# Mixture-of-experts tiles in the order of their first token's batch, with the closing norm of each batch run among the tiles

## What is computed

```python
x = x + layernorm(attention(layernorm(x)))            # x: (8, 512, 128)
# second layer: small 16-head attention, then 8 experts, 2 per token
x2  = h + attn16(rmsnorm(h)) @ w_up                   # h = layernorm(x)
t   = rmsnorm(x2)
w, idx = top2(softmax(t @ router_w))                  # idx: 2 of 8 experts
y   = sum_k w[k] * ((silu(t @ w1[e_k]) * (t @ w3[e_k])) @ w2[e_k])
out = x + layernorm(x2 + y)
```

## Time and profile before

| | us |
|---|---|
| median of 3 runs | 778.08 (777.09 to 778.49) |
| profiled execution | 779.29 |
| its span, first to last instruction | 777.3 |
| PE busy | 660.4 (85%) |
| DVE busy | 503.1 (65%) |
| ACT busy | 396.0 (51%) |
| POOL busy | 355.9 (46%) |
| mean granted TensorE clock | 0.95 |

### The profile page before, as it was taken

One profiled execution on the slowest core, in us unless ns is written; L12 is line 12 of the kernel. 1 busy time (PEld: TensorE's weight loads), 2 busy tenths in 40 slices (PEclk: granted clock), 3 DMA queues, 4 the chain that ended last, 5 costly groups with the idle time before them and its releaser, 6 DMA issues.

```text
span 777.3 us, 15273 instructions
## 1 busy us (share of the span) xinstructions
PE 660.4 (85%) x4861; PEld 394.9 (51%) x4914; DVE 503.1 (65%) x1623; ACT 396.0 (51%) x792; POOL 355.9 (46%) x398
## 2 busy tenths in 40 slices
PE   7976899999899799899989988979879799999900
PEld 3434456466466456546646644545534366666600
DVE  7465866968968677786876876766715144444456
ACT  3243376566476467456646635544521265655515
POOL 4150290391582566349147351640134155555565
PEclk9999799999999999999989999999989999999955
DMA  6101001001001000000100100100025332322163
GB/s 179 43 0 28 1 1 29 1 1 31 27 1 28 29 2 21 29 8 1 35 22 1 28 30 2 29 28 2 1 87 142 71 82 77 82 76 72 51 240 94
DMA packets 38008, 33.27 MB, mean 43 GB/s; under 512 B 6384, under 2 KB 33072, under 8 KB 37920
## 3 DMA queue, kind: packets, MB, share of 16 engines
q1 hardware_dynamic: 33616, 23.39, 11.3%
q0 software_dynamic: 4320, 8.92, 3.5%
HBM read 17.09 MB, written 12.01 MB: 37 GB/s over the span
## 4 chain that ended last, share of the span: by engine, by line
PE 51%; DVE 19%; POOL 14%; issue 9%; ACT 3%; SPq 2%; DMA 2%; another core or an unknown queue 1%; DVEq 0%; POOLq 0%; ACTq 0%
PE wide L979 8%; PE small L803 6%; PE small L758 5%; DVE nmax L1268 5%; PE wide L778 5%; PE small L995 4%; PE small L790 3%; PE small L820 3%; PE small L762 2%; PE small L849 2%; PE wide L733 2%; PE wide L783 2%; PE small L986 2%; POOL k_rows L1181 2%; DVE a_st L1249 2%
## 5 line engine op out<-in xcount | busy, mean ns | idle before, releaser
L1268 DVE TENSOR_REDUCE nmax<-small 128x1 f32<-128x512 f32 (+3 forms) x352 | 217.0, 637 | 66.2 <-PE small L762 46.9
L1077 ACT ACTIVATE pT<-wide 128x1024 f32<-128x1024 f32 x160 | 159.2, 1021 | 72.0 <-PE wide L783 57.5
L758 PE MATMUL small<-kz,qT 128*128 128x256 bf16 (+3 forms) x503 | 123.1, 306 | 22.1 <-DVE nmax L1268 15.4
L1197 POOL DMA_INDIRECT token_rows<-m_row,place_u x64 | 63.0, 984 | 122.3 <-DVE place_u L1473 85.7
L778 PE MATMUL wide<-qT,kz 128*128 128x384 bf16 (+3 forms) x492 | 95.4, 306 | 9.4 <-DVE qT L1414 7.6
L1215 POOL DMA_INDIRECT result_rows<-pT,dest x71 | 68.0, 957 | 67.8 <-issue 38.4
L803 PE MATMUL small<-pT,v_pad 128*5 128x512 f32 (+3 forms) x1024 | 82.0, 461 | 5.3 <-issue 5.3
L762 PE MATMUL small<-future_sb,idb 128*128 128x128 bf16 (+2 forms) x328 | 78.1, 238 | 0.6
L979 PE MATMUL wide<-kz,pT 128*128 x142 | 74.7, 608 | 1.4 <-ACT pT L1110 1.3
L758 PEld LDWEIGHTS small<-kz,qT 128*128 128x128 bf16 x512 | 43.9, 99 | 56.1 <-DVE nmax L1268 30.0
L1528 DVE TENSOR_TENSOR pT<-pT,wide 128x256 f32<-128x256 f32 x71 | 29.9, 421 | 61.2 <-ACT pT L1116 55.3
(11 more groups left out here) (200 smaller groups left out, 1248.4 us busy)
## 6 DMA issues: line engine op xcount, KB each, us to landing
pT<-token_rows SPq DMA_DIRECT2D x71, 65.0 KB
kz<-k_all SPq DMA_DIRECT2D x32, 128.0 KB, 2.4
kz<-result_rows SPq DMA_DIRECT2D x16, 256.0 KB, 5.5
x<-L_attn_x SPq DMA_DIRECT2D x8, 256.0 KB, 3.6
kz<-L_ffn_w SPq DMA_DIRECT2D x2, 1024.0 KB, 6.9
out<-x SPq DMA_DIRECT2D x8, 256.0 KB, 2.2
result_rows<-pT,dest POOLq DMA_INDIRECT x71
token_rows<-m_row,place_u POOLq DMA_INDIRECT x64
```

Source lines behind the costliest of these rows:

```text
L758: pe.matmul(bank[:, at:at + keys], qT1[:, m.parity, g, tile * P:(tile + 1) * P], kz[:, m.parity, g, r, 0:keys], start=(r == r0), stop=Fals ...
L1077: act.activation(pT[:, g % 2, s, :], wide[:, w % 2, :], ACT.Exp, scale=SCALE_B)\
L1197: pool.indirect_dma_start(token_rows[:, :], bass.IndirectOffsetOnAxis(ap=place_u[:, n, t:t + 1], axis=0), m_row[:, n, t, :], None).then_in ...
L1268: ins = dve.tensor_reduce(nmax[:, tile, g * R + r0:g * R + r0 + heads], bank[:, 0:heads * (tile + 1) * P].rearrange("p (h k) -> p h k", h= ...
```

## The change

The tile slots are ordered by the batch in which their first row was written, and by expert within a batch. To know this, the totals per expert are kept after each batch (`totals`, one more small copy in `f_rank`). The tables now work on 8 x 8 begun-tile counts, give each of the 71 slots on its own partition, and PE turns the two columns into rows (two transposes), from which DVE copies them for the registers. At most `8 * (b + 1) + 7` slots precede the end of batch b, so its results are complete after that many tiles.

The closing stage of a batch is cut into pieces that stand at fixed steps behind this number (the lags in the diff). Each engine's step list has them between its own tile parts: on DVE between `take_dest` and `gated`, on ACT between `rows_turned` and `silu_of`, on POOL behind `send_result`, on SP behind `load_rows`. Loads of batches 0 to 5 and stores of the same batches are cut into quarters of 64 KB; batches 6 and 7 load and store whole, behind the last tile. `yin` moves out of the keys' memory, where the expert weights lie, into four other tensors.

```diff
+LOAD_AT, PAIR_AT, SUM_AT, MEAN_AT, POW_AT, SHIFT_AT, NORM_AT, OUT_AT, STORE_AT = 12, 11, 13, 16, 17, 19, 20, 25, 34
+def tiles_before_end_of(b):
+    return NE * (b + 1) + NE - 1
+def due(n, lag):
+    for b in range(NB):
+        if tiles_before_end_of(b) + lag == n:
+            return b
+    return None
+def among_tiles(b):
+    return tiles_before_end_of(b) + LOAD_AT < TILES
+def last_steps(body):
+    for n in range(TILES + 1, tiles_before_end_of(NB - 1) + STORE_AT + 1):
+        body(n)
...
 # SP
-            tile_steps(lambda s: load_rows(s + 2), read_rows)
-            for i in range(BUFS):
-                sp.wait_ge(y_out[i], 16 * len(range(i, TILES, BUFS)))
+            def load_results(b, t):
+                if t == 0:
+                    for i in range(BUFS):
+                        sp.wait_ge(y_out[i], 16 * len(range(i, tiles_before_end_of(b), BUFS)))
...
+            def batch_step(n):
+                for t in range(NT):
+                    if due(n, STORE_AT + t) is not None:
+                        store(due(n, STORE_AT + t), t)
+                    if due(n, LOAD_AT + t) is not None:
+                        load_results(due(n, LOAD_AT + t), t)
...
 # POOL
-            tile_steps(lambda s: send_result(s + -1))
+            def batch_step(n):
+                if due(n, PAIR_AT) is not None:
+                    add_pair(due(n, PAIR_AT))
+                if due(n, POW_AT) is not None:
+                    invert(due(n, POW_AT))
+            def tile_step(s):
+                send_result(s + -1)
+                batch_step(s.n)
...
 # DVE
+                        dve.tensor_copy(totals[:, f.n, :], bank[:, NT * NE:(NT + 1) * NE])
...
+            def add_results(b):
+                dve.wait_ge(pair_sum, b + 1)
+                dve.tensor_tensor(yin[b][:, 0, :, :], yin[b][:, 0, :, :], res[:, b, :, :], ALU.add).then_inc(y_sum, 1)
...
+            def batch_step(n):
+                if due(n, SUM_AT) is not None:
+                    add_results(due(n, SUM_AT))
+                for half in range(2):
+                    if due(n, SUM_AT + 1 + half) is not None:
+                        half_stats(due(n, SUM_AT + 1 + half), half)
+                if due(n, MEAN_AT) is not None:
+                    mean_and_var(due(n, MEAN_AT))
+                if due(n, SHIFT_AT) is not None:
+                    place_norm(due(n, SHIFT_AT))
+                if due(n, OUT_AT) is not None:
+                    finish(due(n, OUT_AT))
+            def tile_step(s):
+                if (s + 2).exists():
+                    take_dest(s + 2)
+                batch_step(s.n)
+                for part, tile in ((gated, s + 1), (result, s + -1)):
+                    if tile.exists():
+                        part(tile)
...
 # ACT
+            def batch_step(n):
+                for t in range(NT):
+                    if due(n, NORM_AT + t) is not None:
+                        normalise_results(due(n, NORM_AT + t), t)
```

More of the change, by code:

```diff
@@ L706, in read_rows @@
             def read_rows(first, count):
-                rows.update(enumerate(read_table(sp, row_u, first, count, NE * REGION + (SPARE - 1) * P), first))
+                rows.update(enumerate(read_table(sp, read_u, first, count, NE * REGION + (SPARE - 1) * P), first))
             sp.wait_ge(pad_in, 16 * NE)
@@ L942, in body @@
                                       start=False, stop=False, skip_group_check=True)
-                        full(ring, step, pe.matmul(bank[:, 0:NT * NE], ones[:, :],
+                        full(ring, step, pe.matmul(bank[:, 0:(NT + 1) * NE], ones[:, :],
                                                    sel_before[:, :, :].rearrange("p t e -> p (t e)"),
@@ L1128, in _ @@
             tile_steps(tile_step)
-            for b in range(NB):
-                par = b % 2
-                rstd, shift = ((a_rstd, a_nb), (p_rstd, p_m2))[par]
-                act.wait_ge(final_shift, b + 1)
-                for t in range(NT):
-                    last = act.activation(yin[:, b, 1, t, :], yin[:, b, 0, t, :], ACT.Identity, bias=shift[:, t:t + 1],
-                                          scale=rstd[:, t:t + 1])
-                last.then_inc(final_norm, 1)
+            last_steps(batch_step)
         @block.gpsimd
@@ new lines, in _ @@
+            table(dve.tensor_tensor(begun[:, :, :], by_batch(tiles_by[:, NE:NE + n_at]), by_batch(tiles_by[:, 0:n_at]),
+                                    ALU.subtract))
+            table(dve.tensor_tensor(le[:, :, :, :], begun[:, :, :].unsqueeze(2).to_broadcast([P, NB, NE, NE]),
+                                    up_to_sb[:, :, :].unsqueeze(1).to_broadcast([P, NB, NE, NE]), ALU.mult))
+            table(dve.tensor_reduce(by_batch(ends[:, :]), le[:, :, :, :], AX, ALU.add))
+            table(dve.tensor_reduce(sums_at[:, :], by_batch(tiles_at[:, 0:n_at]), AX, ALU.add))
@@ new lines, in _ @@
+            table(dve.tensor_tensor(by_batch(ends[:, :]), by_batch(ends[:, :]),
+                                    sums_at[:, :].unsqueeze(2).to_broadcast([P, NB, NE]), ALU.add))
+            table(dve.tensor_tensor(from_end[:, 1:n_at + 1], tiles_at[:, 1:n_at + 1], ends[:, :], ALU.subtract))
+            table(dve.tensor_tensor(change[:, 1, :], from_end[:, 1:n_at + 1], from_end[:, 0:n_at], ALU.subtract))
+            table(dve.tensor_tensor(at_end[:, :], ends[:, :], row_of[:, 0:1].to_broadcast([P, n_at]), ALU.is_le))
@@ new lines, in _ @@
+            table(dve.tensor_tensor(parts_of[:, :, :], change[:, :, :],
+                                    at_end[:, :].unsqueeze(1).to_broadcast([P, 2, n_at]), ALU.mult))
+            table(dve.tensor_reduce(sums[:, :], parts_of[:, :, :], AX, ALU.add))
+            table(dve.tensor_scalar(tile_row[:, :], sums[:, 0:1], float(REGION // P), row_of[:, 0:1], ALU.mult, ALU.add))
+            table(dve.tensor_tensor(tile_row[:, :], tile_row[:, :], sums[:, 1:2], ALU.add))
+            table(dve.tensor_scalar(tile_at[:, 0:1], tile_row[:, :], float(P), None, ALU.mult))
```

175 lines of the change are left out of this document (102 added, 73 removed).

## The result

| | before | after |
|---|---|---|
| median of 4 runs, us | 778.17 (777.09 to 778.49) | 790.15 (787.41 to 791.36) |
| profiled execution (span), us | 779.29 (777.3) | 790.03 (788.2) |

A forecast was written before the change was run, and what follows sets the result against it. PE was taken to bound the tile stage, with pure tail behind it. Tail -18.3, DVE waits +8.3 and attention +0.5 give -9.5 us on 779.3, so 769.8, median 768.6; range 761 to 776, 8 in 10.

The forecast's parts named there:

- The tail: Behind the last send: closing work of most batches moves among the tiles, leaving 17.75 us for 36.05, 18.3 us less.
- 1.45 for a power: On POOL in the tail: the duration taken for each batch's power operation, 1.45 us.
- Two late inputs on DVE: Tile stage: DVE waits for POOL's pair sums and powers, so PE loses 0.8 + 5 x 1.5 = 8.3 us.
- Sums at 1.61 us: Tile stage: if all six POOL sums were slowed by port sharing with DVE, 2.1 us more, time 770.7.
- SP's queue: Tile stage: at 0.50 us per quarter issue SP works 12.1 of 13.1 us, so its waits cost nothing.
- about 2 us per transfer: Quarter loads and stores: each transfer pays this fixed part, quarters four times; hidden in SP's lead, so the sum is unchanged.
- Tables and attention: Before the first tile: new table chain some 0.7 us later but hidden, extra attention copies 0.5 us; together 0.5 more.
- the padding hides it, with 6 us to spare: Start: the new table chain, some 0.7 us later, still ends ahead of SP's first tile load, issued behind the padding.
- The copies per batch in attention: Attention stage: one more DVE copy of 0.19 us per batch costs 0 to 1.5 us, taken as 0.5.
- the late inputs cost PE nothing: Rival for the tile stage: the lags leave room enough, so DVE's waits cost PE nothing; 760.3 us, chance 0.17.
- SP as the bound: Rival for the tile stage: quarters cost 1.21 us each to issue, SP is too slow; some 794 us, chance 0.06.

The follow-up runs named there:

- e1_even: The changed kernel with one word of padding, so PE's table of experts begins at word 72, not 71; 773.15 us, ratio 0.9923.
- e3_all_last: e1_even with all nine lags 57 steps larger, so that every closing piece stands behind the last tile; 793.88 us, ratio 1.0189.
- r_even: e1_even run again, on one chip with r_after and r_before; 771.10 us, ratio 0.9929.
- r_after: The changed kernel run again with its trace, on the same chip as r_even and r_before; 786.22 us, ratio 1.0119.
- r_before: The kernel before, unchanged, profiled once on the same chip as r_even and r_after; 781.79 us.
- e2_before_odd: The kernel before with only PE's table of experts moved by one word, to an odd word; 793.44 us, ratio 1.0171.

## Why the prediction was wrong

**The tail: right.** Forecast 17.75 us from the end of the last send, or 18.7 from its start; measured 18.1 from its start, and 18.1 in e1_even. Most of the 0.6 is the power of batch 5, which took 1.04, not 1.45. Two shifts behind powers took 1.2 us instead of 0.16, but they end with POOL's sum, for which DVE waits next anyway, so they cost nothing. The timeline of the tail of after:

```profile
771.09 1.04 POOL L1299 TENSOR_TENSOR p_rstd<-p_ve,neg_half 128x4 f32<-128x4 f32 x1
772.12 1.25 POOL L1291 TENSOR_TENSOR qT<-qT 128x512 f32<-128x512 f32 x1
772.16 1.23 DVE L1660 SCALAR_TENSOR_TENSOR p_m<-p_mv,p_rstd 128x4 f32<-128x4 f32 x1 [3.19 <-POOL p_rstd L1299]
...
780.65 1.39 POOL L1299 TENSOR_TENSOR p_rstd<-p_ve,neg_half 128x4 f32<-128x4 f32 x1 [2.33 <-DVE p_ve L1655]
...
783.95 0.69 DVE L1665 TENSOR_TENSOR x<-x,qT 128x512 f32<-128x512 f32 x1 [1.72 <-ACT qT L1189]
```

The last addition ends at 784.64, 3.5 us ahead of the span's end, as in the forecast.

The forecast's 1.45 for a power was read where DVE was adding at the same time. In the tail of e3_all_last POOL has been idle for 2.33 us ahead of both of these powers; the second starts 0.17 us into an addition of DVE, the first doesn't:

```profile
750.45 1.04 POOL L1300 TENSOR_TENSOR a_rstd<-a_ve,neg_half 128x4 f32<-128x4 f32 x1 [2.33 <-DVE a_ve L1656]
...
754.89 0.68 DVE L1666 TENSOR_TENSOR x<-x,a_p_sb 128x512 f32<-128x512 f32 x1
755.06 1.39 POOL L1300 TENSOR_TENSOR p_rstd<-p_ve,neg_half 128x4 f32<-128x4 f32 x1 [2.33 <-DVE p_ve L1656]
```

**Two late inputs on DVE: the mechanism right, the sum right by luck.** 8.3 forecast, 8.4 measured between e1_even and e3_all_last. The waits stand where they were laid out: in after DVE stood 1.3, 1.8, 1.8, 3.2, 1.6 and 1.8 us ahead of the sums (1.3 to 1.6 forecast) and 1.5, 1.6, 1.1, 1.1 and 1.6 ahead of the shifts (1.5 forecast), each released by POOL. Their prices for PE were 0.6 for 0.8 in batch 0 and 1.6 for 1.5 in batch 1. But batch 3 took 4.2, 1.93 of DVE's wait there being POOL's own stand ahead of a send, and the kernel used for comparison has 3.1 us of long steps that e1_even hasn't. The two happened to offset each other.

**Sums at 1.61 us: they didn't come.** The six sums among the tiles took 1.27 to 1.28. The sentence of the Trainium skill (Advanced Engine Details and Errata, "VectorE Performance Modes") that VectorE's two-port instructions and GpSimd's block each other would have added 2.1 us, if it had held for every sum. It held for none of these, and none of them starts while an addition of 128x512 runs on DVE, which stands waiting for it. Elsewhere the traces agree that the two engines hold each other up; which port does it they don't show. The shift L1660 at 772.16, of 128x4, started 0.04 us behind POOL's sum, took 1.23 us, where the earlier trace rows has 0.16, and ended at 773.39, as the sum did (773.37); the same pair stands at 777.07 and 777.12, 1.22 us. The other way round, the sum of 1.61 in the earlier trace rows starts 0.20 us into DVE's addition, as the powers of 1.39 and 1.45 do.

**SP's queue: right.** Two quarter loads took 0.83 to 1.01 us in the rows around 658, 0.42 to 0.5 each, where I took 0.50. No idle time of PE or DVE in the tile stage was released by a row load, and no sum of a pair among the tiles waited for its quarters. The section of the Trainium skill that the forecast named for about 2 us per transfer (DMA: Bandwidth & Descriptors, "Anatomy of one DMA") describes transfers issued by GpSimd, and the quarters go out from SP; the sum didn't hang on it.

**Tables and attention: the step that failed.** It reads "the padding hides it, with 6 us to spare". Two things were wrong. First, I set the new chain's end against SP's first row load, and left out what stands behind the tables on PE: register load and 26 products. The spare time there was the 2.38 us of idle ahead of L973, in the trace of before, not 6. The new chain's own length was right: without the wait the copy would have ended at 605.94, 7.1 us behind the totals, where the old table ended 6.6 behind them. Then the wait adds 4.4, the load 4.0 and the products 1.8: 0.5 + 4.4 + 4.0 + 1.8 - 2.4 = 8.3, the start's difference of 8.2 but for rounding. Second, the step said nothing of where the new table lies. It asked how long the table takes to make, and not what reads it. The three loads per run were a row of the trace of before (1.7 to 2.1 us each, two of them in the very stage that PE bounds), and a change of their operand was in the diff: the forecast should have named them, and bounded their price. This term, absent from the sum, measured +15.0 us (e1_even against after by pieces; r_even against r_after 15.1 by medians, 13.6 by pieces). The whole then reads: tail -18.9, odd word +15.0, closing pieces among the tiles +8.4, start apart from the odd word +5.0, attention +2.4, and -1.1 between the tile stage of before and that of e3_all_last; together +10.8, the difference of the spans (10.9) but for rounding. Of the +5.0 the cause of 4.4, the late copy, stays open.

The Trainium skill (Runtime: NRT & Kernel Launch, "Instruction fetch mechanics") gives some 200 ns per register for the loads that the runtime puts around a kernel, which read registers from HBM. By that figure 24 registers would be 4.8 us, an estimate. The rows here, of loads from SBUF, show 5857 / 24 = 244 ns from an odd word and 1825 / 24 = 76 ns from a multiple of four words: two prices, where the page has one between them.

**The copies per batch in attention** can't be told: +2.4 in after, but +0.6 in e1_even, and 595.9 in r_after against 598.5 in r_before. The stage scatters by more than the 0.5 I gave it.

**Rivals.** None named this. That the late inputs cost PE nothing is refuted by the steps above. SP as the bound, the one on the slower side, was wrong in mechanism. With the even word the time, 773.15 and 771.10, lies inside the range given (761 to 776), 2.5 to 4.6 us over the forecast, about what the start lost.

## What to carry to other kernels

When a change rebuilds a table, follow it to its readers: how many registers each engine loads from it, at what address, and where in its instruction stream. Before calling a new piece hidden, take the chain on the engine that bounds the next stage, not the queue with the widest gap. A piece that hangs on another engine in an in-order list costs its wait each time; often the shorter way is to do it on the waiting engine, where here 0.68 us fitted into a gap of 0.84.

## What the hardware showed

- **A load of registers on PE** from SBUF (24, 24 and 23 of them) took 5.53 to 6.04 us from one or three words past a multiple of four words (16 bytes), in the 9 loads of after, r_after and e2_before_odd, and 1.65 to 2.24 from such a multiple, in the 9 of before, e1_even and r_even. Two words past it was not tried.
- **The clock behind a hole**: behind 5.0 us without matmuls PE's up products took 2.07 us, twice the 1.02 of the full clock, for one to two steps. The holes of the short loads (0.81 and 1.85 us of idle PE in e1_even) left the stretches in which they lie at a granted clock of 1.00. Behind the 2.28 us for which PE stood for batch 3's sum in e1_even an up product took 1.91, and the stretch from 715 to 725 has a clock of 0.83.
- **POOL beside an addition of DVE**: a power of 128x4 on POOL took 1.02 to 1.05 us whenever no 128x512 addition of DVE was running as it started (63 powers of the 160 in all traces, one of them behind 2.33 us of idle), and 1.38 to 1.54 where it started with 0.51 us or more of such an addition still to run (95 powers; the other two, with 0.16 us left, took 1.06 and 1.07). All eight powers of before are of the second kind (1.42 to 1.49). The same goes for POOL's sends: the six of after that start 0.13 us into DVE's sum with the residual took 1.41 to 1.42, not 0.96.
- **DVE beside a sum of POOL**: a shift of 128x4 that starts 0.04 to 0.05 us behind POOL's sum ends with it, after 1.22 to 1.23 us instead of 0.16 (after, e1_even, e3_all_last).
- **Chips differ**: on three of five the attention stage was 25 us shorter, the kernel before took 746 to 748 us instead of 777 to 778, and the wait of 4.4 us was absent. The tile stage was shorter too in the two versions that ran on both kinds: 126.4 to 126.5 us against 132.1, and 123.6 against 128.8. Only times of one chip can be compared.
